# The closing of a graph kernel's program: engines meet on semaphores without GpSimd's drain

## The chip, the core and the metric

The kernel runs on one NeuronCore of a Trainium2 chip. The core has five engines that run side by side: TensorE (PE, with its weight loads as PEld), VectorE (DVE), ScalarE (ACT), GpSimd (POOL) and SyncE (SP). Each takes its own list of instructions in order through a sequencer of its own, which the profile writes with a q (POOLq, SPq). SyncE here only starts plain DMA transfers and waits for semaphores. GpSimd here starts indirect transfers, which gather or scatter rows of HBM by a list of row numbers. The metric is the device time of one execution in microseconds (us), lower is better. The profiler's span runs from the program's first instruction to its last; the metric is a little longer than the span.

## The reference, cut to what matters

The work is one attention step over the edges of a graph, a residual and a layer norm, all in float32. There are 100,000 nodes with 128 features and 25,000 edges, sorted by their receiving node.

```
edge_feat = concatenate([h[dst], h[src], rel_pos, distance])      # per edge, 260 numbers
x      = silu(edge_feat @ W1 + b1)
x      = silu(x @ W2 + b2)
scores = x @ W3 + b3
alpha  = exp(scores - segment_max) / (segment_sum(exp) + 1e-12)   # over the edges of one node
msg    = h[src] @ Wv * (alpha * node_weight[src])
out    = h + segment_sum(msg)                                     # one row per node
result = layernorm(x + out)                                       # 100,000 rows of 128
```

A node that receives no edge has a result that is the layer norm of 2x alone. Only rows of nodes that receive an edge need the long way.

## The kernel before

**Tiling.** The 25,000 edges are padded to 49 groups (G) of 512 edges, each of four tiles (TPG) of 128. The 100,000 rows are taken as 49 dense blocks (NB) of 2,048.

**Stages.** The first stage gathers the sending rows of every edge, computes their part of the first layer and sorts the edges; its results lie in HBM as rec_d. The second stage runs from the step called B0: it gathers the receiving rows (hk) and the records (region) by the sorted order, computes the scores, the weights within a segment and the messages, and leaves the finished rows of each group in hk. Beside both stages runs the dense part: a block is loaded into xin, normed by VectorE and ScalarE, and stored to the output tensor out_rows, whether or not its nodes receive an edge.

**Scatters.** When all dense blocks are stored, GpSimd writes the rows of the nodes that receive an edge over them. For each group it issues four indirect transfers (`scatter`, the transfer itself on L418), 196 in all, from hk by the row numbers in sidx_t. Each group signals a semaphore of the ring `scattered`. At last there is the repair of segments that cross tiles: VectorE, TensorE and ScalarE make yfix (in the tile xin), and two more scatters write it by fixi, signalling `fix_out`. Those two are the last work of the program.

**What waits for the scatters.** SyncE has nothing left to issue then, and waits for them in its last lines:

```
            for r in range(SC_SEMS):
                sp.wait_ge(scattered[r], 16 * TPG * len(range(r, G, SC_SEMS)))    # L407
            sp.wait_ge(S["fix_out"], 32)                                          # L408
```

**The closing.** The whole program stands in one block (`nc.Block`, entered through the ExitStack of L131, so the block's closing carries the line L131 in the trace). When the block ends, each engine branches to its own few closing instructions. The opening of the program, on L1101, has a meeting of the same make as the closing of before. In the closing the built program of before has these instructions, in each engine's order ("gather" and "release" are the two semaphores of the meeting):

```
ACT, PE, DVE, SP (each):  DRAIN            waits for release = 0, then adds 1 to gather
                          EVENT_SEMAPHORE  waits for release >= 1, then takes 1 from it
POOL:                     DRAIN            no wait on a semaphore, no signal
                          EVENT_SEMAPHORE  waits for gather >= 4, then takes 4 from it
                          EVENT_SEMAPHORE  adds 4 to release
```

So GpSimd is the one that lets the others go, and it does so behind its own DRAIN.

Of the kernel before, what the change touches and what calls it, by code (L numbers as in the profile page):

```python
# [120 lines left out]
def gnn_kernel(nc, x, xw, snd_nat, rcv_nat, id_nat, signs, iota, ef_flat, w1, b1, w2, b2, w3, b3, wv, eye, out):  # L121
# [9 lines left out]
    with ExitStack() as ctx:  # L131
# [124 lines left out]
        y_out = [sem(f"y_out{r}") for r in range(Y_SEMS)]  # L256
        scattered = [sem(f"scattered{r}") for r in range(SC_SEMS)]

        block = ctx.enter_context(nc.Block())

        def wait(eng, s, n):
            if n > 0:
# [848 lines left out]
```

## Time and profile before

| | before |
|---|---|
| time, median of 3 runs | 1004.3 us (1003.87 to 1004.84) |
| the profiled execution, its own time | 1004.35 us |
| its span, first to last instruction | 1002.5 us |
| what lies around the span | 1.85 us |
| busiest engine | POOL, 754.2 us (75%) |

The profiled execution's own time is within 0.05 us of the median, so its trace can stand for the runs. The table's last row but one is the difference of the two rows above it. In the profile's page the span is also cut into 40 slices of 25 us each, with a digit for the busy tenths of each engine; an engine's last digits tell whether it works at the end of the program.

### The profile page before, as it was taken

The page shows a single profiled execution, that of the slowest core. Times are in us where ns is not written, and L with a number is a line of the kernel's source. Part 1 is how long each engine was busy: PE and PEld are TensorE (multiplying, and loading weights), DVE is VectorE, ACT ScalarE, POOL GpSimd, SP SyncE. Part 2 cuts the span into 40 slices and gives each one's busy share as a digit, 9 for nine tenths or more (in the row PEclk, how much of TensorE's full clock was granted, in tenths as well). Part 3 has the DMA queues.
Part 4 walks back from the last instruction along what each step waited for, and adds up shares of the span by engine and source line. Part 5 has one row for each costly group of instructions (what it writes and reads, how often), then busy time and mean ns, then how long its engine had stood idle before and what let it go on. Part 6 is the DMA issues. An engine that isn't in the chain of part 4 may idle for free.

```text
span 1002.5 us, 11553 instructions
## 1 busy us (share of the span) xinstructions
PE 609.8 (61%) x2783; PEld 421.0 (42%) x2783; DVE 583.1 (58%) x2276; ACT 523.5 (52%) x1168; POOL 754.2 (75%) x790
## 2 busy tenths in 40 slices
PE   1889999999604445787776867787767755000000
PEld 0656766666402223555554545555545554000000
DVE  7977877664432637788998798944243476400000
ACT  0356665555513657778799888964444435100000
POOL 6777777777777777777777777777777777777775
PEclk9999999999998777878988998898898967555555
DMA  6799999979955877787777967642222211211110
GB/s 209 227 308 323 328 329 330 313 217 345 339 174 163 289 247 258 255 296 252 256 282 246 324 227 271 224 123 79 75 78 72 68 48 50 70 44 47 47 45 32
DMA packets 77915, 198.24 MB, mean 198 GB/s; under 512 B 19007, under 2 KB 49409, under 8 KB 65304
## 3 DMA queue, kind: packets, MB, share of 16 engines
q1 hardware_dynamic: 49560, 134.47, 38.1%
q0 software_dynamic: 28288, 63.03, 21.5%
q8 instruction: 23, 0.38, 0.2%
q14 instruction: 44, 0.36, 0.1%
HBM read 106.74 MB, written 92.26 MB: 198 GB/s over the span
## 4 chain that ended last, share of the span: by engine, by line
POOL 32%; issue 23%; PE 20%; ACT 13%; DVE 7%; SPq 2%; DMA 1%; POOLq 1%; ACTq 0%; DVEq 0%
POOL hk L414 19%; POOL out_rows L418 13%; ACT xin L472 6%; PE bank L624 4%; PE bank L649 3%; PE bank L618 3%; PE bank L611 3%; PE bank L640 2%; PE bank L626 2%; ACT zs L515 2%; ACT hk L524 2%; DVE dst L895 1%; ACT L500 1%; ACT x L505 1%; ACT L510 1%
## 5 line engine op out<-in xcount | busy, mean ns | idle before, releaser
L472 ACT ACTIVATE xin<-xin,drs 128x128 f32<-128x128 f32 x637 | 258.3, 486 | 45.2 <-DVE drs L880 45.1
L418 POOL DMA_INDIRECT out_rows<-hk,sidx_t x196 | 191.4, 977 | 59.7 <-issue 59.4
L414 POOL DMA_INDIRECT hk<-in_xw,snd_t x196 | 188.7, 963 | 62.0 <-issue 58.2
L414 POOL DMA_INDIRECT region<-rec_d,id_t x196 | 186.1, 950 | 59.7 <-issue 58.2
L414 POOL DMA_INDIRECT hk<-in_x,kg_t x196 | 185.9, 948 | 59.7 <-issue 57.3
L895 DVE BATCH_NORM_STATS2 dst<-xin 128x6 f32<-128x256 f32 x392 | 137.0, 414 | 53.3 <-DMA xin<-in_x 52.8
L571 PE MATMUL bank<-w1b,region 128*128 128x128 f32 x392 | 148.7, 483 | 14.2 <-ACT region L482 7.4
L624 PE MATMUL bank<-hkT,w1a 128*128 128x512 f32 x98 | 67.3, 776 | 123.7 <-issue 85.6
L571 PEld LDWEIGHTS bank<-w1b,region 128*128 128x128 f32 x392 | 100.0, 315 | 33.1 <-ACT region L482 8.6
L505 ACT ACTIVATE x<-bank,bcol 128x512 f32<-128x512 f32 x49 | 33.4, 682 | 129.3 <-PE bank L626 129.3
L649 PE MATMUL bank<-wvh,zs 128*128 128x128 f32 x392 | 64.5, 314 | 58.9 <-ACT zs L515 57.5
L972 DVE TENSOR_TENSOR hk<-bank,hk 128x512 f32<-128x512 f32 x49 | 33.6, 686 | 100.9 <-PE bank L649 100.9
L624 PEld LDWEIGHTS bank<-hkT,w1a 128*128 128x128 f32 x98 | 18.7, 219 | 160.1 <-issue 156.0
L649 PEld LDWEIGHTS bank<-wvh,zs 128*128 128x128 f32 x392 | 54.0, 213 | 70.5 <-ACT zs L515 70.5
L524 ACT ACTIVATE hk<-hk,ers 128x128 f32<-128x128 f32 x196 | 79.8, 484 | 2.3 <-DVE ers L880 2.3
L482 ACT ACTIVATE region<-bank 128x512 f32<-128x512 f32 x49 | 28.9, 590 | 96.8 <-PE bank L578 96.8
L963 DVE TENSOR_SCALAR m_q<-bank,kcol,acol 128x128 f32<-128x128 f32 x196 | 73.3, 401 | 0.3
L640 PE MATMUL bank<-m_q,region 128*128 128x128 f32 x392 | 69.0, 334 | 0.0
L578 PE MATMUL bank<-ident,hk 128*128 128x128 f32 x196 | 54.3, 433 | 22.5 <-DMA w<-hk 15.8
L611 PE MATMUL bank<-x,wz 128*16 128x128 f32 x392 | 62.3, 312 | 5.1 <-ACT x L500 4.6
L640 PEld LDWEIGHTS bank<-m_q,region 128*128 128x128 f32 x392 | 64.2, 248 | 1.0 <-issue 0.7
L618 PE MATMUL bank<-x,w2s 128*128 128x512 f32 x98 | 61.4, 711 | 0.2 <-ACT x L505 0.2
(179 smaller groups left out, 918.3 us busy)
## 6 DMA issues: line engine op xcount, KB each, us to landing
xin<-in_x SPq DMA_DIRECT2D x49, 1024.0 KB, 7.2
out_rows<-xin SPq DMA_DIRECT2D x49, 1024.0 KB, 4.8
rec_d<-hk SPq DMA_DIRECT2D x49, 514.0 KB, 6.6
hk<-in_xw,snd_t POOLq DMA_INDIRECT x196, 5.4
hk<-in_x,kg_t POOLq DMA_INDIRECT x196, 3.2
region<-rec_d,id_t POOLq DMA_INDIRECT x196, 2.9
out_rows<-hk,sidx_t POOLq DMA_INDIRECT x196, 2.2
ef_d<-hk SPq DMA_DIRECT2D x9, 196.0 KB, 3.4
```

What stands on the lines that cost most here:

```text
L414: pool.indirect_dma_start(out=to, out_offset=None, in_=frm, in_offset=bass.IndirectOffsetOnAxis(ap=index, axis=0)).then_inc(done, 16)
L418: pool.indirect_dma_start(out=out, out_offset=bass.IndirectOffsetOnAxis(ap=index, axis=0), in_=frm, in_offset=None, bounds_check=N - 1, oo ...
L472: ins = nc.scalar.activation(xin[:, j % X_RING, n, :], xin[:, j % X_RING, n, :], ACT.Identity, bias=drs[:, j % 2, 1, n:n + 1], scale=drs[: ...
L524: ins = nc.scalar.activation(hk[:, g, q, :], hk[:, g, q, :], ACT.Identity, scale=ers[:, b % 2, 0, n:n + 1], bias=ers[:, b % 2, 1, n:n + 1])
L571: pe.matmul(to, hsT[:, j % 2, q * P:(q + 1) * P], w1b[:], start=True, stop=False)
L611: ins = pe.matmul(bank[3][0:BT, 0:P], wz[:, BT - 1 - n:2 * BT - 1 - n], x2[:, q * P:(q + 1) * P], start=(n == 0), stop=(last and q == TPG ...
L618: pe.matmul(bank[2][:], w2s[:], x1[:], start=True, stop=True).then_inc(S["mm2_done"], 1)
L624: pe.matmul(bank[1][:], w1a[:], hkT[:, g % 2, :], start=True, stop=False, skip_group_check=True)
L640: ins = pe.matmul(bank[5][:, q * P:(q + 1) * P], rr[:, g % R_RING, q, H:2 * H], m_q[:, g % 2, q, :], start=True, stop=True)
L649: ins = pe.matmul(bank[6][:, q * P:(q + 1) * P], zs[:, q * P:(q + 1) * P], wvh[:], start=True, stop=True)
L895: ins = vec.bn_stats(dst[:, n:n + 2, :].rearrange("p j w -> p (j w)"), xin[:, j % X_RING, n:n + 2, :].rearrange("p j h -> p h j"))
L963: ins = vec.tensor_scalar(m_q[:, g % 2, q, :], bank[4][:, q * P:(q + 1) * P], kcol[:, t:t + 1], acol[:, b % 2, n:n + 1], ALU.is_equal, ALU ...
```

## The change

The block is made with an option that takes GpSimd's DRAIN out of its closing. Nothing else of the source is touched.

```diff
-        block = ctx.enter_context(nc.Block())
+        block = ctx.enter_context(nc.Block(no_gpsimd_drain=True))
```

The instructions that compute and transfer are the same, in the same order, on each of the five engines; only the block's closing differs. The built program of the changed kernel has there:

```
ACT, PE, DVE, SP (each):  DRAIN            no wait, no signal
                          EVENT_SEMAPHORE  waits for release = 0, then adds 1 to gather
                          EVENT_SEMAPHORE  waits for release >= 1, then takes 1 from it
POOL:                     EVENT_SEMAPHORE  waits for gather >= 4, then takes 4 from it
                          EVENT_SEMAPHORE  adds 4 to release
```

GpSimd's DRAIN is gone. The other four keep theirs, and signal with an instruction of its own behind it, so each has one instruction more. GpSimd's two stay as they were. The waits of SyncE on L407 and L408 stand ahead of its DRAIN, as before.

## Rows read from the trace of the kernel before

**Rows 1.** The page, its head: span, busy time, 40 slices of each engine.

```profile
span 1002.5 us, 11553 instructions
...
PE 609.8 (61%) x2783; PEld 421.0 (42%) x2783; DVE 583.1 (58%) x2276; ACT 523.5 (52%) x1168; POOL 754.2 (75%) x790
...
DVE  7977877664432637788998798944243476400000
ACT  0356665555513657778799888964444435100000
POOL 6777777777777777777777777777777777777775
```

**Rows 2.** Busy time of stretches at the end; columns as its head says.

```profile
core 0: us, PE busy (x) PEld busy (x) DVE busy (x) ACT busy (x) POOL busy (x), PEclk, DMA share, GB/s
...
900.00:996.30 96.30, 0.00 (x0) 0.00 (x0) 0.00 (x0) 0.00 (x0) 73.36 (x76) 0.50 0.13 45
996.30:997.40 1.10, 0.00 (x0) 0.00 (x0) 0.00 (x0) 0.00 (x0) 0.00 (x0) 0.50 0.03 2
997.40:1002.50 5.10, 0.00 (x0) 0.00 (x0) 0.00 (x0) 0.00 (x0) 0.00 (x0) 0.50 0.00 0
```

**Rows 3.** The chain that ended last, 976 to 1002.5: start, us, what.

```profile
979.61 0.02 issue
979.63 0.03 POOLq L418
...
980.88 0.02 issue
980.91 1.25 POOLq L131
982.16 0.30 issue
...
993.96 0.97 POOL out_rows L418
994.93 0.30 issue
995.23 0.97 POOL out_rows L418
```

**Rows 4.** Line L418, the scatters: duration ns min/median/max, first and last start.

```profile
L418 POOLq MOVE  x198: 29/29/35, 682.0 to 979.6; - x198
...
L418 POOL DMA_INDIRECT out_rows<-xin,fixi x2: 971/972/972, 994.0 to 995.2; - x2
```

**Rows 5.** What SyncE waited for from 990 us on: total, times, longest.

```profile
SPq L408 <- DMA out_rows<-xin,fixi: 7.5, 1, 7.5
SPq L131 <- PEq L131: 4.9, 1, 4.9
```

**Rows 6.** Output tensor out_rows from 990 us on: issue to landing.

```profile
DMA to landing us min/median/max: 2.1/2.1/2.2
```

**Rows 7.** SyncE's wait on L408: duration ns, first and last start.

```profile
L408 SPq EVENT_SEMAPHORE  x1: 28/28/28, 997.3 to 997.3; - x1
```

**Rows 8.** Line L131, the block's closing: duration ns, first and last start.

```profile
L131 POOLq EVENT_SEMAPHORE  x2: 17/17/17, 1002.4 to 1002.4; - x2
L131 PEldq DRAIN  x1: 742/742/742, 873.2 to 873.2; - x1
L131 DVEq DRAIN  x1: 201/201/201, 877.5 to 877.5; - x1
L131 ACTq DRAIN  x1: 907/907/907, 877.7 to 877.7; - x1
L131 POOLq DRAIN  x1: 21410/21410/21410, 980.9 to 980.9; - x1
L131 SPq COMPARE_BRANCH  x1: 38/38/38, 997.4 to 997.4; - x1
L131 SPq DRAIN  x1: 7/7/7, 997.6 to 997.6; - x1
L131 SPq EVENT_SEMAPHORE  x1: 17/17/17, 1002.5 to 1002.5; - x1
```

**Rows 9.** Line L1101, the program's opening: the same columns.

```profile
L1101 POOLq EVENT_SEMAPHORE  x2: 17/17/17, 0.5 to 0.6; - x2
...
L1101 POOLq DRAIN  x1: 188/188/188, 0.3 to 0.3; - x1
...
L1101 POOL MEMSET const-uint8-127<- x1: 119/119/119, 0.3 to 0.3; 128x1 uint8 x1
...
L1101 PEldq EVENT_SEMAPHORE  x1: 51/51/51, 0.7 to 0.7; - x1
```

## The prediction

> **What bounds the kernel now.** I read the page's head first, to see who works at the end. In the 40 slices the last five digits of VectorE and ScalarE are 0, while GpSimd's row holds 7s and then a 5 [rows 1]. The kernel ends on GpSimd alone. The busy time of the last stretches says it more sharply: from 900.0 to 996.3 us the only busy engine is GpSimd, with 76 scatters and 73.36 us; from 996.3 to 997.4 no engine is busy and a little data moves; from 997.4 to the end, 5.1 us, nothing at all is busy and the DMA engines carry 0 GB/s [rows 2]. So the last 5 us are not work. Anything that shortens them shortens the program, provided that the metric does not wait for the same thing elsewhere.
>
> Then I read the chain that ended last, for the order of events. The last two scatters start at 993.96 and 995.23 and are recorded as 0.97 us each, so the last ends at 996.20 [rows 3]. The line of the scatters shows that GpSimd's sequencer is far ahead of them: its last MOVE, which belongs to the last scatter, stands at 979.6, and that scatter starts at 995.2, 15.6 us later [rows 4]. Behind that MOVE the sequencer meets the closing's DRAIN at 980.91 [rows 3]. It lasts 21,410 ns [rows 8], so it ends at 980.91 + 21.41 = 1002.32. That is 6.12 us after the last scatter's recorded end.
>
> What did SyncE, which watches for the landing, see? From issue to landing the last scatters take 2.1 to 2.2 us [rows 6], so the last lands at 995.23 + 2.1 = 997.3. SyncE's wait on L408 ends just there, at 997.3 [rows 7]. It branches into the closing at 997.4 and its DRAIN, 7 ns, stands at 997.6; then it has nothing to do until its last instruction at 1002.5 [rows 8]. The view of waits gives this as 4.9 us on L131 and names PE's sequencer as the one that ended it [rows 5]. That name has to be read with care: the wait is for the release semaphore, which GpSimd alone raises. PE's closing DRAIN was over at 873.2 + 0.7 us, ScalarE's at 878.6 [rows 8]. The real releaser is the GpSimd instruction at 1002.4, and what held that one is the DRAIN which ended at 1002.32. All four others had signalled by 997.6.
>
> **The change, part by part.**
>
> *Removed: GpSimd's DRAIN.* With it gone, the sequencer reaches its EVENT_SEMAPHORE for gather >= 4 at about 980.9 and waits there for SyncE, the last of the four. Nothing is queued behind it on GpSimd but the release. The twelve scatters still to run are already handed over, as the 15.6 us lead shows (12 times the spacing of 1.27 us is 15.3). The release is thus set by SyncE, at 997.6. Nothing before that point changes: the instructions ahead of the closing are the same, and the scatters, spaced 995.23 - 993.96 = 1.27 us, go on at their pace.
>
> *Added: one EVENT_SEMAPHORE on each of the other four.* Those of TensorE, VectorE and ScalarE run near 878 us, about 119 us ahead of need; they cost nothing, and would cost 0.02 to 0.05 us each if they stood last. SyncE's stands on the path. An EVENT_SEMAPHORE is 17 ns [rows 8]; the two of GpSimd at the opening are about 0.1 us apart [rows 9], so I take 0.05 us for it, with bounds of 0.02 and 0.2.
>
> *Kept: the handing over.* From the end of GpSimd's DRAIN to the end of the span it takes 1002.5 - 1002.32 = about 0.2 us. The opening has the same steps: its DRAIN ends at 0.3 + 0.19 = 0.5 and PE's last instruction starts at 0.7, again 0.2 us [rows 9]. I take 0.2, bounds 0.15 and 0.4.
>
> *The sum.* SyncE is done at 997.6, plus 0.05, plus 0.2, gives an end of 997.85 instead of 1002.5. The span falls by 4.65 us to 997.85. If the 1.85 us around the span stay, the profiled execution's 1004.35 becomes 999.7. The median of the runs is 0.05 below that execution, so the time is 999.65 us, a gain of 0.46%. By the bounds the end lies between 997.77 and 998.2, and the time between 999.6 and 1000.0. The runs of before spread over about 1 us; with that the likeliest case's own range is 999.1 to 1000.4. About 0.2%, 2.0 us, is what a measurement of this kernel can tell from no change, and 4.65 us is above it.
>
> *Where the unknown lies.* The trace does not say what the DRAIN did from 996.2 to 1002.3. It was not waiting for data: 0 GB/s moved from 997.4 on [rows 2], and the last landing was at 997.3. At the opening, GpSimd's DRAIN lasts 0.19 us in all, with memsets of 0.12 us still running as it starts [rows 9]: a drain with no transfer ahead of it costs less than 0.2 us. So the 6.1 us belong to transfers having been issued, or to the DRAIN's own handling of them. If GpSimd must do that work anyway before the runtime calls the execution over, it is still to be paid. Its price is between 0 (nobody asks) and 7.1 us (from the last scatter's start at 995.23 to 1002.32). I take 0, since all that the program itself needs is in place at 997.3 and since the metric holds only 1.85 us outside of the span, too little for a long procedure.
>
> A rule of the Trainium skill can be held against this. DMA: Bandwidth & Descriptors, "Anatomy of one DMA — SWDGE (gpsimd) path", puts the fixed cost of one GpSimd transfer at about 2.0 us, most of it the receipt of the write. The landing of 2.1 us agrees [rows 6]. If the drain waited only for transfers to complete, by that rule it would be over at about 997.3 and its removal would be worth nothing; the row of the drain, which ends 5 us later, says otherwise [rows 8], and the sum goes by the row.
>
> **The rivals.**
>
> *The drain moves outside.* The runtime's own closing also makes engines meet, and if it asks GpSimd to finish, the removed wait reappears behind the span. The span falls to 997.85 all the same, but GpSimd is done at 1002.32 as before, for what it does began when the scatters ended; the handing over within the program, 0.2 us, may be saved. The time is then 1004.35 less 0 to 0.2: 1004.2. For it: 1.85 us lie outside the span, and something fills them. Against it: a stretch as short as this leaves little room for steps between all engines, and part of it may lie ahead of the span. A middle way, in which the metric's last 1.85 us overlap the drain in part, ends between 999.7 and 1004.2. Chance 0.25.
>
> The Trainium skill speaks for this rival. Runtime: NRT & Kernel Launch, "The ~15µs preamble/postamble breakdown", lists a sync barrier of about 1.5 us behind the kernel which waits for all engines, and VectorE: DVE Perf Modes, "The DRAIN you can't avoid", says that such runtime code has DRAINs on all five engines. No row here shows whether the metric includes them.
>
> *The drain is paid late and whole (the slower side).* The 6.1 us may be the handling that a DRAIN starts, and not something under way since the last scatter. Asked for by the runtime only after the meeting at 997.85, it would end at 997.85 + 6.12 = 1003.97, and the time would be 1005.8, 1.5 us over before. If its price counts from the last scatter's start, 7.1 us, the time is 1006.8, slower by 0.25%. It shows as slower when the price is over 6.1 + 0.5 = 6.6 us. For it: the drain's record is one unbroken piece that ends 5 us after all data landed. Against it: the metric would have to hold it, and GpSimd is free from 996.2 on. Chance 0.09, of which I give half to each side of that point.
>
> *The option does nothing on the path.* If GpSimd's sequencer could not pass its closing semaphores until its queue had emptied, the release would still come at 1002.4, and the time would be 1004.3. Against it: the sequencer's MOVEs and waits run 15.6 us ahead of the scatters [rows 4], and the MOVE is no different from a semaphore in that. Chance 0.03.
>
> **How the numbers follow.** The full gain has 0.63; the middle and outside case 0.25, of which 0.03 falls in the middle and still shows as faster; late and whole 0.09; nothing on the path 0.03. Faster: 0.63 + 0.03 = 0.66. Slower: 0.045, rounded to 0.04. Same: 0.30, the rest. The time is that of the full gain, 999.65, given as 999.6. The full gain alone holds less than 8 in 10, so the range has to reach to the outside case: 999.1 to 1004.8 takes in all of it and the run-to-run spread, and leaves out the late case (0.09) and a small tail below.
>
> **What the changed profile would show.** No DRAIN of POOLq on L131. SyncE's DRAIN at about 997.6 as before, GpSimd's two EVENT_SEMAPHOREs at about 997.7, not 1002.4, and a span of about 997.9. SyncE's wait on L131 falls from 4.9 to about 0.2 us. The landing on L408 stays at about 997.3. If the first rival holds, all of this is seen too, and only the part around the span grows, from 1.85 to about 6.3 us; with the late drain it grows to 8 or more. If the option does nothing on the path, GpSimd's EVENT_SEMAPHOREs still stand at 1002.4. The prediction would also be wrong if the scatters themselves changed their pace or their landing, for which I see no cause.

## The result: 5 us less, and the profile after

The changed kernel takes 999.33 us (median of 6 runs, 998.69 to 1001.02) against 1004.36 us for the kernel before in the same timings (6 runs, 1003.87 to 1005.06). The ratio is 0.9947, with a 95% interval of 0.9938 to 0.9957: 0.53% faster. Applied to the 1004.3 us of before, the ratio gives 998.98 us, just below the 999.1 us at which the forecast range began. The two medians by themselves are 5.03 us apart. A second timing of the same kernel gave 0.9957 (0.9944 to 0.9971), which is told below.

The closing, first. These are lines of L131 of the changed kernel (duration ns min/median/max, first and last start), to be held against [rows 8]:

```profile
L131 PEldq EVENT_SEMAPHORE  x2: 51/51/51, 875.0 to 997.6; - x2
L131 DVEq EVENT_SEMAPHORE  x2: 21/21/21, 878.7 to 997.6; - x2
L131 ACTq EVENT_SEMAPHORE  x2: 17/17/17, 879.6 to 997.6; - x2
L131 SPq EVENT_SEMAPHORE  x2: 17/17/17, 997.4 to 997.6; - x2
L131 POOLq EVENT_SEMAPHORE  x2: 17/17/17, 997.5 to 997.5; - x2
...
L131 SPq DRAIN  x1: 7/7/7, 997.4 to 997.4; - x1
```

GpSimd's DRAIN of 21,410 ns is not there, and its two EVENT_SEMAPHOREs stand at 997.5 instead of 1002.4. They follow SyncE's first one at 997.4 within 0.1 us. The other three engines' first ones are at 875.0 to 879.6, about 118 us ahead of need.

What SyncE waited for from 880 us on, beside [rows 5] (total, times, longest):

```profile
SPq L408 <- DMA out_rows<-xin,fixi: 7.5, 1, 7.5
SPq L131 <- PEq L131: 0.2, 1, 0.2
```

The wait for the landing is unchanged at 7.5 us. The wait for the release went from 4.9 to 0.2 us. The busy time of the last stretches tells the rest; [rows 2] had 5.1 us of nothing in the last one:

```profile
core 0: us, PE busy (x) PEld busy (x) DVE busy (x) ACT busy (x) POOL busy (x), PEclk, DMA share, GB/s
900.00:995.90 95.90, 0.00 (x0) 0.00 (x0) 0.00 (x0) 0.00 (x0) 73.06 (x76) 0.50 0.13 45
995.90:997.10 1.20, 0.00 (x0) 0.00 (x0) 0.00 (x0) 0.00 (x0) 0.09 (x1) 0.50 0.02 2
997.10:997.60 0.50, 0.00 (x0) 0.00 (x0) 0.00 (x0) 0.00 (x0) 0.00 (x0) 0.50 0.00 0
```

The last landing, SyncE's wait on L408, and the scatters ahead of it:

```profile
L408 SPq EVENT_SEMAPHORE  x1: 28/28/28, 997.1 to 997.1; - x1
```

```profile
L418 POOLq MOVE  x198: 29/29/35, 681.8 to 979.4; - x198
...
L418 POOL DMA_INDIRECT out_rows<-xin,fixi x2: 971/972/972, 993.7 to 995.0; - x2
```

So the account of the profiled execution is: span 1002.5 to 997.6 us, 4.9 us less. Of that, 0.2 us lie ahead of the closing (the landing at 997.1 instead of 997.3 [rows 7]), and 5.2 - 0.5 = 4.7 us in the closing itself. Around the span the time stayed: the execution took 999.43 us, 1.83 us over its span, against 1.85 before. The removed wait did not come back there. No row shows whether what the DRAIN did is now done after the program, or not at all.

### The profile page after: what moved, and what is told of

The parts are those of the page before. It is cut to its first block, busy times and chain, and to the rows that moved or that the text cites. A ratio compares the mean times of both kernels' runs of the same rounds, so it can differ in the third digit from the quotient of the medians.

```text
span 997.6 us, 11556 instructions
## 1 busy us (share of the span) xinstructions
PE 610.1 (61%) x2783; PEld 419.3 (42%) x2783; DVE 582.9 (58%) x2276; ACT 523.5 (52%) x1168; POOL 754.0 (76%) x790
## 4 chain that ended last, share of the span: by engine, by line
POOL 39%; issue 22%; PE 16%; DVE 11%; ACT 10%; SPq 2%; DMA 1%; POOLq 1%; ACTq 0%; DVEq 0%
POOL hk L414 23%; POOL out_rows L418 12%; ACT xin L472 4%; POOL region L414 3%; PE bank L624 3%; PE bank L649 3%; DVE dst L895 3%; PE bank L618 2%; PE bank L640 2%; PE bank L611 2%; ACT zs L515 2%; ACT hk L524 1%; PE bank L626 1%; DVE m_q L963 1%; DVE hk L972 1%
## 5 line engine op out<-in xcount | busy, mean ns | idle before, releaser
L418 POOL DMA_INDIRECT out_rows<-hk,sidx_t x196 | 191.2, 975 | 59.7 <-issue 59.1
L624 PE MATMUL bank<-hkT,w1a 128*128 128x512 f32 x98 | 70.5, 809 | 124.2 <-issue 86.5
L649 PEld LDWEIGHTS bank<-wvh,zs 128*128 128x128 f32 x392 | 56.0, 220 | 71.7 <-ACT zs L515 71.7
L640 PE MATMUL bank<-m_q,region 128*128 128x128 f32 x392 | 64.5, 317 | 0.0
L640 PEld LDWEIGHTS bank<-m_q,region 128*128 128x128 f32 x392 | 59.0, 230 | 1.0 <-issue 0.7
```

The costliest lines, as they stand in the source:

```text
L418: pool.indirect_dma_start(out=out, out_offset=bass.IndirectOffsetOnAxis(ap=index, axis=0), in_=frm, in_offset=None, bounds_check=N - 1, oo ...
L624: pe.matmul(bank[1][:], w1a[:], hkT[:, g % 2, :], start=True, stop=False, skip_group_check=True)
L640: ins = pe.matmul(bank[5][:, q * P:(q + 1) * P], rr[:, g % R_RING, q, H:2 * H], m_q[:, g % 2, q, :], start=True, stop=True)
L649: ins = pe.matmul(bank[6][:, q * P:(q + 1) * P], zs[:, q * P:(q + 1) * P], wvh[:], start=True, stop=True)
```

## The experiments

All but the last two (a_fifth and z_before) ran on three other chips, on which the kernel before itself took 1188 to 1200 us, with its runs 1 to 2% apart. Their medians say little about 5 us; the rows of their drains and closings say much, and each ratio is to the kernel before on the same chip.

### The drain put back by hand

```diff
         for k in range(2):
             scatter(yfix[:, k, :], fixi[:, k:k + 1], S["fix_out"])
+        pool.drain()
```

The closing stays that of the changed kernel; all edits below start from it too.

> GpSimd's DRAIN is written by hand behind its last scatter, the closing stays that of the change. If the DRAIN alone is what cost the 4.7 us, this is as slow as before, 1004.3 us within 0.3 (the drain ends about 6.1 us after the last scatter's recorded end). If the new form of the meeting (signals by EVENT_SEMAPHORE) had a part in the gain, it is faster than before by that part.

Measured: ratio 1.0002 to before (0.9963 to 1.0041), no gain. Line L463, the drain:

```profile
L463 POOLq DRAIN  x1: 7454/7454/7454, 1179.7 to 1179.7; - x1
```

GpSimd's last scatters in the same kernel (start us, us):

```profile
1178.78 0.97 POOL L418 DMA_INDIRECT out_rows<-xin,fixi  x1 [0.30 <-issue]
1180.06 0.97 POOL L418 DMA_INDIRECT out_rows<-xin,fixi  x1 [0.31 <-issue]
```

The drain ends at 1179.69 + 7.45 = 1187.14, which is 6.1 us after the last scatter's recorded end at 1181.03, as in the kernel before. SyncE saw the landing at 1182.2 and the span ends at 1187.4, so the closing takes 5.2 us, again as before. The new form of the meeting has no part in the gain that these rows could show; the DRAIN is what costs.

### When is the price due?

One kernel lets GpSimd wait for the landing and then drain. The other lets ScalarE first copy a tile 12 times behind the landing, and GpSimd drains after that.

```diff
+        pool.wait_ge(S["fix_out"], 32)     # the second kernel: pool.wait_ge(S["late"], 12)
+        pool.drain()
```

```diff
+            act.wait_ge(S["fix_out"], 32)
+            for n in range(12):
+                nc.scalar.activation(x2[:], x1[:], ACT.Copy).then_inc(S["late"], 1)
+                act.wait_ge(S["late"], n + 1)
```

> GpSimd waits for the landing of the last scatters (about 997.2 us) and drains only then. If the 6.1 us are something that goes on in GpSimd since the last scatter, the drain still ends at about 1002.2 and lasts 5.0 us, and the time is 1004.2 to 1004.4. If a DRAIN starts the work when it is handled, it lasts 6.1 us from 997.2 and ends at 1003.3, and the time is about 1005.3. If it only waits for transfers to complete, it lasts under 0.2 us, and the time is about 999.5.

> As the one before, but ScalarE first does 12 copies of 128x512 one after the other from the landing on, about 10 us, and GpSimd drains only then, at about 1007. If the 6.1 us go on in GpSimd by themselves, they are over by then and the drain lasts under 0.2 us, time about 1009 to 1010. If a DRAIN starts them, it lasts 5 to 6.1 us as before, time about 1015.

Line L464, the drain of the first kernel and the landing beside it:

```profile
L464 POOLq DRAIN  x1: 6108/6108/6108, 1183.7 to 1183.7; - x1
```

```profile
L408 SPq EVENT_SEMAPHORE  x1: 28/28/28, 1183.7 to 1183.7; - x1
```

The same two lines of the second kernel:

```profile
L464 POOLq DRAIN  x1: 6108/6108/6108, 1189.2 to 1189.2; - x1
```

```profile
L408 SPq EVENT_SEMAPHORE  x1: 28/28/28, 1181.2 to 1181.2; - x1
```

Both last 6108 ns, to the nanosecond: one begins at the landing, the other about 8 us after it. All transfers have landed in both, so no transfer is waited for. The 6.1 us are something that a DRAIN starts when GpSimd comes to it, and not something under way since the last scatter. I call it the work of the DRAIN; what it consists of, no row shows. The theory of work in the background is refuted. The first kernel's median was 1189.55 against 1188.27 us of before (ratio 0.9998, 0.9962 to 1.0034): the medians cannot tell the 1 us more that was expected, but the rows do. From the landing to the end of the span it took 1190.0 - 1183.7 = 6.3 us, where the drain put back by hand took 5.2. The second kernel ran once, 1197.31 us; my 1015 us had assumed a chip like the first one, and the 12 copies took 7.9 us, not 10.

### Two drains, one of them behind two transfers

```diff
+        pool.drain()
         pool.wait_ge(S["fix_res"], 1)
         for k in range(2):
             scatter(yfix[:, k, :], fixi[:, k:k + 1], S["fix_out"])
+        pool.drain()
```

> The changed kernel with two drains by hand on GpSimd: one ahead of the last two scatters, one behind them. Both earlier drains lasted 6.11 us from when GpSimd came to them, at the landing and 8 us later alike. If 6.1 us is the price of each DRAIN, both cost it: the last two scatters start 6.1 us after the scatter before them, the time is about 12.2 us over the changed kernel. If the price goes with the transfers issued since the last drain (794 at the first, 2 at the second), the second costs under 0.3 us and the sum is about 6.4 us.

The scatters of GpSimd around the two drains, the drains' own lines, and SyncE's wait for the landing:

```profile
1185.01 0.97 POOL L418 DMA_INDIRECT out_rows<-hk,sidx_t  x1 [0.30 <-issue]
1192.74 0.97 POOL L418 DMA_INDIRECT out_rows<-xin,fixi  x1 [6.76 <-issue]
1194.02 0.97 POOL L418 DMA_INDIRECT out_rows<-xin,fixi  x1 [0.30 <-issue]
```

```profile
L460 POOLq DRAIN  x1: 6804/6804/6804, 1185.1 to 1185.1; - x1
```

```profile
L464 POOLq DRAIN  x1: 3154/3154/3154, 1193.1 to 1193.1; - x1
```

```profile
L408 SPq EVENT_SEMAPHORE  x1: 28/28/28, 1196.1 to 1196.1; - x1
```

The first drain ends at 1185.13 + 6.80 = 1191.9, 5.95 us behind the scatter ahead of it, and opens a gap of 6.76 us. It stands behind 784 transfers: the trace has 786 in all, and the 794 of my expectation was a miscount. The second drain ends at 1193.07 + 3.15 = 1196.2, only 1.2 us behind the last scatter's recorded end. The price is therefore not the same for each DRAIN. My second case had under 0.3 us for this drain, since it forgot the landing: SyncE saw the last scatter land at 1196.1 (the line of L408 above), 0.1 us ahead of the drain's end. So I read two parts in a drain: it waits for what has not landed, and it does work that depends on the transfers issued. The first part rests on this one coincidence. The two do not add up. With the drain put back by hand it ended 6.1 us after the last scatter's recorded end, at 1187.1, and not 6.1 us after the landing at 1182.2.

The time was 1204.12 us (ratio to before 1.0032, 0.9995 to 1.0068) against 1197.88 us of the changed kernel on the same chip (0.9974, 0.9944 to 1.0004). That is 6.2 us more, but with these intervals the times alone would hardly exclude the 12.2 us of a fixed price; the rows do. The Trainium skill (DMA: Bandwidth & Descriptors, "Anatomy of one DMA — SWDGE (gpsimd) path") has about 2.0 us fixed for a GpSimd transfer. The second drain, which ends 2.2 us after the start of the scatter ahead of it, agrees with that; the first, 6.9 us after such a start, does not.

### Drains early in the program

```diff
         pool.wait_ge(S["snd_in"], 16)
+        pool.drain()
         for kind, g in pool_plan():
+            if kind == "hs" and g in (1, 2, 8, 32):
+                pool.drain()
...
+        pool.drain()
```

> The changed kernel with drains by hand on GpSimd ahead of its first gather (no transfer issued), after 4, 8, 32 and 128 gathers, and at the end. A fixed price per DRAIN once a transfer has been issued gives under 0.2 us for the first and about 6.1 us for each of the others. A fixed price whatever was issued gives 6.1 us for the first too. A price by the count since the last drain gives 0, then values that grow from 4 transfers to 660: in the ratio of the counts 4, 4, 24, 96.

The lines of the drains (ahead of any transfer; the four between; the last):

```profile
L422 POOLq DRAIN  x1: 41/41/41, 2.8 to 2.8; - x1
```

```profile
L425 POOLq DRAIN  x4: 7880/11273/18165, 4.9 to 192.4; - x4
```

```profile
L466 POOLq DRAIN  x1: 5460/5460/5460, 1205.5 to 1205.5; - x1
```

With no transfer issued the drain costs 41 ns. For the others the record's own length is not the price, since its start is not the moment at which GpSimd has done with the transfer ahead; so I take the time from the end of that transfer. For the four between it is 4.8 us behind 4 gathers, 4.1 behind the next 4, 2.6 behind 24, 7.9 behind 96. For the first of them, and for the one behind 96, the rows are (start us, us, idle before):

```profile
7.66 1.13 POOL L414 DMA_INDIRECT hk<-in_xw,snd_t  x1 [0.30 <-issue]
14.30 1.10 POOL L414 DMA_INDIRECT hk<-in_xw,snd_t  x1 [5.52 <-issue]
...
197.46 0.95 POOL L414 DMA_INDIRECT hk<-in_xw,snd_t  x1 [0.30 <-issue]
207.09 0.95 POOL L414 DMA_INDIRECT hk<-in_xw,snd_t  x1 [8.68 <-PE bank L582]
```

The last drain of the four ends at 192.4 + 13.9 = 206.3, and the gather ahead of it at 198.4. All four may contain the landing of gathers, which was not there for the 6108 ns.

The drain at the end of the program has to be read in the same way, and the 5.46 us that my next expectations take for it are a misreading. These are the last scatter and the line of the sequencer's MOVEs:

```profile
1203.86 0.97 POOL L418 DMA_INDIRECT out_rows<-xin,fixi  x1 [0.30 <-issue]
```

```profile
L418 POOLq MOVE  x198: 2/29/1397, 839.7 to 1204.1; - x198
```

The MOVE of the last scatter is recorded at 1204.1, after the scatter itself has started at 1203.9. The sequencer's records stand late here, and so does the start of the drain's, 1205.5. From the last scatter's recorded end, 1204.83, to the drain's end, 1205.5 + 5.46 = 1210.9, it is 6.1 us. That is what the kernels with 786 transfers and no drain between have, though here the drain before stood only 658 transfers back. Proportion to the count since the last drain is refuted (24 gives less than 4, and 658 as much as 786), and so is one fixed price.

### Does the price go in a sawtooth?

These two leave out the scatters of the last 10 or 20 groups (40 or 80 transfers); the rows of those nodes keep the dense result. GpSimd drains once, after the landing.

```diff
-                else:
+                elif g < G - 10:                       # 20 for 10 in the second, here and below
...
-                sp.wait_ge(scattered[r], 16 * TPG * len(range(r, G, SC_SEMS)))
+                sp.wait_ge(scattered[r], 16 * TPG * len(range(r, G - 10, SC_SEMS)))
...
+            pool.wait_ge(S["fix_out"], 32)
+            pool.drain()
```

> The last 10 groups' 40 scatters are left out (their rows keep the dense result), and GpSimd drains once, after the landing of the last two scatters: 746 transfers were issued. The rows so far: 6.108 us behind 786 transfers, 5.95 behind 784, 5.46 behind 658 since the drain before, 7.9 behind 96, 2.6 behind 24. They fit 0.0785 us for each transfer in a ring that is cleared every 118 transfers (786 = 6 x 118 + 78, 658 = 5 x 118 + 68). By that 746 = 6 x 118 + 38 gives 3.0 us. A fixed price gives 6.1 us, one that goes with the whole count 5.8 us.

> As the one before, with the last 20 groups' 80 scatters left out: 706 transfers. By the ring of 118 transfers 706 = 5 x 118 + 116 gives 9.1 us, more than behind 786 although fewer were issued. A fixed price gives 6.1 us, one that goes with the whole count 5.5 us.

The drains, of the first and of the second:

```profile
L464 POOLq DRAIN  x1: 2389/2389/2389, 1129.1 to 1129.1; - x1
```

```profile
L464 POOLq DRAIN  x1: 8722/8722/8722, 1093.7 to 1093.7; - x1
```

Fewer transfers, and the drain goes from 6.11 us (786) down to 2.39 (746) and up to 8.72 (706). A fixed price and one that grows with the whole count are refuted. A price that rises and falls back in teeth was forecast to give 3.0 and 9.1, and fits in kind. The 2.39 may even be too low. In the second kernel the drain's record starts with the landing (L408 at 1093.7), as it did in the kernel that drained behind the landing (both 1183.7). In the first it starts 0.4 us later than this line, and ends 2.8 us after it:

```profile
L408 SPq EVENT_SEMAPHORE  x1: 28/28/28, 1128.7 to 1128.7; - x1
```

The law stays open. My fit rested in part on the misread 5.46 us: teeth of 118 transfers with 0.0785 us for each give 5.3 us for the 658 transfers of the kernel before, which cost 6.1. The slope between 746 and 786 transfers is (6.108 - 2.389) / 40 = 0.093 us, or 0.08 if the first is taken as 2.8, and these three counts do not fix the width of a tooth. Both kernels ran once. That a ring of descriptors is cleared when full is my reading and was not shown.

### How large is the gain?

The changed kernel was timed four more times, and a copy of the kernel before once as a control.

> The changed kernel once more, unaltered, for the size of the gain. If the sum of the prediction is complete (the drain's 4.65 to 4.9 us and nothing else), its median is 999.5 to 999.7 us and the ratio to before is 0.9952 to 0.9954. If the removal also moves something ahead of the closing, as the 0.9947 of the first timing would have it, the ratio stays at or under 0.9947, 5.3 us or more. The last landing, SyncE's wait on L408, would tell it: 997.3 us in the profile of before, 997.1 in that of the change.

> The changed kernel once more, unaltered, for the size of the gain, since the timing before this one had runs spread over 2%. If the sum is complete (a drain handled at 996.2 that ended at 1002.3, against a closing that follows SyncE at 997.4), the ratio is 0.9952 to 0.9954, 4.6 to 4.9 us. If something ahead of the closing also moves, it is 0.9947 or less.

> The changed kernel once more for the size of the gain, in the hope of runs that lie close together. 4.6 to 4.9 us (0.9952 to 0.9954) if the closing is all; 5.3 or more if something ahead of it moves too.

> The changed kernel once more beside a copy of the kernel before. Where a core's closing runs as in the first profiles, the closing gives 4.7 us; where SyncE's last instructions take 0.70 us each, as in the three timings since, it gives 3.5 us. The ratio should be 0.9953 in the one case and 0.9971 in the other.

> A copy of the kernel before, as a control: with nothing changed the ratio is 1, and its distance from 1 shows what this measurement makes of no change. If it is off by 0.0006 or more, the first timing's 5.3 us cannot be told from the 4.7 us of the sum; if it lies within 0.0002, the 0.6 us more would want a cause.

| timing | before, us | changed, us | ratio (95% interval) |
|---|---|---|---|
| first | 1004.36 | 999.33 | 0.9947 (0.9938 to 0.9957) |
| a_again | 1188.27 | 1186.26 | 0.9977 (0.994 to 1.0013) |
| a_third | 1199.88 | 1197.88 | 0.9974 (0.9944 to 1.0004) |
| a_fourth | 1198.78 | 1195.33 | 0.9962 (0.9933 to 0.999) |
| a_fifth | 1004.39 | 999.73 | 0.9957 (0.9944 to 0.9971) |
| z_before, nothing changed | 1004.39 | 1004.3 | 1.0 (0.9991 to 1.0009) |

The three rows in the middle are on the other chips, where each ratio is too wide to tell 3.5 from 4.7 us. SyncE's records are longer there. In a_again (first line) its two EVENT_SEMAPHOREs take 0.70 us each instead of 0.017. The others are SyncE's and GpSimd's in a_third, then GpSimd's in a_again:

```profile
L131 SPq EVENT_SEMAPHORE  x2: 696/697/698, 1183.6 to 1184.3; - x2
```

```profile
L131 SPq EVENT_SEMAPHORE  x2: 21/710/1398, 1199.1 to 1201.2; - x2
L131 POOLq EVENT_SEMAPHORE  x2: 17/17/17, 1198.8 to 1198.9; - x2
```

```profile
L131 POOLq EVENT_SEMAPHORE  x2: 17/17/17, 1183.6 to 1183.7; - x2
```

These long records must be read with care, and the 3.5 us that I expected from them are too simple. In a_third GpSimd has released at 1198.9, while the signal of SyncE that it waited for is recorded at 1199.1. The release stands 0.4 to 0.5 us behind the landing in all five profiles of the changed kernel, the long records or not. What they lengthen is the end of the span, and the time around the span shrinks in exchange. The whole is seen in what it takes from the landing (SyncE's wait on L408) to the end:

| profile | landing, us | to the end of the span | to the end of the execution |
|---|---|---|---|
| before | 997.3 | 5.2 | 7.05 |
| z_before | 996.5 | 5.2 | 7.07 |
| b_drain_back | 1182.2 | 5.2 | 6.97 |
| changed, first timing | 997.1 | 0.5 | 2.33 |
| a_fifth | 996.4 | 0.5 | 2.33 |
| a_again | 1183.2 | 1.8 | 2.79 |
| a_third | 1198.5 | 2.7 | 3.88 |
| a_fourth | 1191.7 | 2.6 | 3.79 |

The last column is the execution's own time less the landing, which counts all of the time around the span as if it stood behind it. By it the change gives 4.7 us in both pairs of the 1004 us timings, 4.2 us in a_again (against b_drain_back) and, against the same 7.0 us, 3.1 to 3.3 in a_third and a_fourth. Why SyncE's last record comes late there is open. It is not the chip alone: with two drains, on the chip of a_third, SyncE's take 17 ns each, and the span ends 0.5 us behind the landing.

The other two timings, the first and a_fifth, lie close together and give 0.9947 and 0.9957, 5.3 and 4.3 us, with 4.8 us in the middle. The control lies at 1.0, and by my own yardstick the 0.6 us that the first timing shows over the closing's 4.7 would then want a cause. But the yardstick was too fine: the control is itself uncertain by 0.0009, 0.9 us, and 4.7 us (0.9953) lies within both intervals. In the profiles what differs besides the closing is where the landing stands, and it stood at 997.3 and at 996.5 with nothing changed.

## Why the prediction was right, and where its range was not

**What bounds the end.** Right: GpSimd's drain alone held the release, and the waits' name for the releaser was to be read through. With the drain out, all that stood behind SyncE's 997.4 was 0.2 us.

**The removed drain.** Forecast 4.65 us in the closing, measured 4.7 in the profiles, and again in a_fifth beside z_before. The handing over was 0.2 us as taken, SyncE's added EVENT_SEMAPHORE under 0.1. The sum gave 999.65 us; the two close timings gave 999.33 and 999.73.

**The price outside the program.** I took 0, and it is 0: 1.83 us lie around the span after, 1.85 before. The rival in which the drain moves outside had 0.25 and fell, though my picture in it (the work is under way since the scatters ended) was wrong as well.

**The slow side.** Its premise was right, its conclusion wrong: the 6.1 us begin when a DRAIN is handled. But nothing within the metric asks for them once the program's own DRAIN is gone.

**The option without effect.** Fell: GpSimd's semaphores were done at 997.5, not 1002.4. Whether they could have passed with scatters still queued this does not show, since the last scatter's record had ended at 996.0.

**The step that failed** is the likeliest case's own range. I let it begin at 999.1 us: the sum's lower bound, 999.6, less half of the 1 us by which the runs of before were spread. The ratio to before made it 998.98. The term mis-sized is this spread: the changed kernel's own runs lie between 998.69 and 1001.02, and the ratio of two timings of the same pair differs by 0.0010, 1 us. A low end of 998.6 would have held both timings (0.9957 x 1004.3 is 1000.0). The mechanism and the terms of the sum held, and chance decided the 0.12 us by which the range was missed: the medians by themselves, 5.03 us apart, would put the time at 999.27, inside it. Nothing in the profile calls for another cause. Where the landing stood varies from execution to execution: 997.3 and 996.5 in the two profiles of before, 997.1 after, and 996.4 in a_fifth:

```profile
L408 SPq EVENT_SEMAPHORE  x1: 28/28/28, 996.4 to 996.4; - x1
```

That is 0.7 us earlier than 997.1, with the very same kernel.

## What to carry to other kernels

Look at what stands behind the last landing: a program that ends on GpSimd's indirect transfers may pay several us for a drain after all its data are home, and here SyncE, which waits for every completion semaphore of the scatters, was enough for the program to end without it. That this is safe in every program was not shown. If a drain has to stay, its price is not to be guessed from another kernel or another count of transfers: 2.4, 6.1 and 8.7 us were seen for three counts in one kernel. Its price is read from the end of the last transfer ahead of it, not from the length of its record (21.4 us here, for 6.1 us behind the last scatter). When a sum is good to 0.1 us, make its range as wide as two timings of one kernel lie apart, not as the sum's own bounds.

## What was not expected

A DRAIN on GpSimd costs 41 ns when no indirect transfer was issued, and 2.39, 8.72 and 6.11 us behind 746, 706 and 786 of them with everything landed, the last to the nanosecond alike in two kernels. Behind 786 transfers it was 6.1 us on every chip where it was seen, and also when four other drains had stood between. The chip seems to matter far more than the change: the kernel before took 1004.4 us in two timings and 1188 to 1200 us in the others, on three chips, where SyncE's first EVENT_SEMAPHORE in the closing took 0.6 to 1.4 us in most profiles. Each of these chips was timed on one occasion only, so that it is the chip, and what in it, was not shown.
